# Scores for the row maximum in two 64-row halves of the array, two units at a time

## The reference

```python
q_lat = einsum('bqhd,hdl->bhql', q, k_eff)            # 16 heads of 8, latent 64
attn  = softmax(causal(q_lat @ c_kv.T / sqrt(8)))
y     = einsum('bhql,hld->bqhd', attn @ c_kv, v_eff)
g     = silu(sum over the 2 best of 8 experts: gate * (gelu(xn w1 + b1) w2 + b2))
x     = x + y * g
```

## Time and profile before

| | us |
|---|---|
| median of 3 runs | 772.93 (767.08 to 774.23) |
| the profiled execution | 773.25 |
| its span, first to last instruction | 771.5 |
| iteration 1 (maximum only) | 41.2 to 95.4 |
| iteration 2 | 95.4 to 160.4 |
| iterations 4 to 7, each | about 82 |
| the exponentials without maxima begin | 648 |

### The profile page before, as it was taken

How to read it: one execution, slowest core, us unless ns; L and a number is a source line. 1 busy time by engine, 2 the same in 40 slices (tenths; PEclk the granted TensorE clock), 3 DMA queues, 4 the chain that set the end, 5 groups by cost and what they waited for, 6 DMA issues and landing times.

```text
span 771.5 us, 14463 instructions
## 1 busy us (share of the span) xinstructions
PE 663.5 (86%) x5682; PEld 458.5 (59%) x5734; DVE 448.1 (58%) x1044; ACT 369.3 (48%) x688; POOL 234.9 (30%) x356
## 2 busy tenths in 40 slices
PE   4177698979999899989998999899998998896875
PEld 2034365537666676657665876576666775555663
DVE  5466357555857576576758575758575654425331
ACT  3502346744556455644556455645564556571210
POOL 5703001222333153124404331423331502224431
PEclk9999889979999999999999999999999999999995
DMA  2732730450035102530044004400341000000000
GB/s 71 135 62 53 120 58 8 98 95 7 8 82 97 36 1 66 88 68 1 28 100 85 8 7 103 105 7 7 87 87 27 2 7 15 21 2 0 1 14 14
DMA packets 31283, 36.31 MB, mean 47 GB/s; under 512 B 4385, under 2 KB 26512, under 8 KB 31216
## 3 DMA queue, kind: packets, MB, share of 16 engines
q1 hardware_dynamic: 31216, 35.39, 22.1%
HBM read 24.44 MB, written 9.96 MB: 45 GB/s over the span
## 4 chain that ended last, share of the span: by engine, by line
PE 64%; DVE 17%; DMA 6%; issue 4%; ACT 4%; POOL 3%; SPq 2%; another core or an unknown queue 0%; POOLq 0%; DVEq 0%; ACTq 0%
PE ps_s L804 8%; PE ps_v L824 8%; PE ps_e L789 5%; DVE cand L1264 5%; DMA kst<-split_scratch 4%; PE ps_a L749 4%; PE ps_e L786 4%; PE ps_c L890 3%; PE ps_c L903 3%; PE ps_a L738 3%; PE ps_a L713 3%; PE ps_s L808 2%; DVE stats L1195 2%; PE ps_c L907 2%; DVE second L1209 2%
## 5 line engine op out<-in xcount | busy, mean ns | idle before, releaser
L1264 DVE TENSOR_REDUCE cand<-ps_s 128x4 f32<-128x512 f32 (+1 forms) x320 | 212.9, 683 | 94.0 <-PE ps_s L808 73.8
L1069 ACT ACTIVATE prob<-ps_e 128x512 f32<-128x512 f32 x320 | 188.2, 597 | 136.8 <-PE ps_e L789 97.2
L804 PE MATMUL ps_s<-kst,qst 96*128 96x128 bf16 (+1 forms) x1024 | 134.2, 249 | 41.8 <-DMA kst<-split_scratch 23.6
L804 PEld LDWEIGHTS ps_s<-kst,qst 96*128 96x128 bf16 x1024 | 81.0, 105 | 100.7 <-issue 52.4
L789 PE MATMUL ps_e<-qst,kst 128*128 128x128 bf16 (+3 forms) x460 | 104.5, 296 | 0.0
L824 PE MATMUL ps_v<-prob,vaug 128*32 128x512 f32 (+3 forms) x1024 | 89.0, 443 | 0.3
L786 PE MATMUL ps_e<-identb,negmask 128*128 128x256 bf16 (+1 forms) x320 | 83.3, 260 | 6.0 <-ACT prob L1069 5.8
L624 POOL TENSOR_TENSOR second<-second,upmask 128x512 f32<-128x512 f32 x42 | 53.1, 1274 | 34.6 <-PE ps_c L890 34.6
L789 PEld LDWEIGHTS ps_e<-qst,kst 128*128 128x128 bf16 x512 | 50.6, 99 | 5.6 <-issue 0.3
L587 POOL CAST mparts<-nm 128x32 bf16<-128x32 f32 x16 | 3.4, 212 | 157.9 <-DVE nm L1271 157.9
L890 PE MATMUL ps_c<-second 128*128 128x128 f32 x336 | 46.0, 280 | 1.0 <-DVE second L1319 1.0
(11 more groups left out here) (301 smaller groups left out, 1076.6 us busy)
## 6 DMA issues: line engine op xcount, KB each, us to landing
qst<-split_scratch SPq DMA_DIRECT2D x48, 192.0 KB
kst<-split_scratch SPq DMA_DIRECT2D x144, 64.0 KB
split_scratch<-qparts SPq DMA_DIRECT2D x8, 384.0 KB, 2.5
split_scratch<-kparts SPq DMA_DIRECT2D x8, 384.0 KB, 2.5
xn<-in_L_attn_x_dram SPq DMA_DIRECT2D x8, 256.0 KB, 3.1
x_res<-in_L_attn_x_dram SPq DMA_DIRECT2D x8, 256.0 KB, 6.8
out_dram<-second SPq DMA_DIRECT2D x7, 256.0 KB, 2.4
max_scratch<-mrow SPq DMA_DIRECT2D x16, 96.0 KB, 1.7
```

The source lines that it names most:

```text
L804: last = mm(ps_s[:, bank, w * n:w * (n + 1)], q[0:MAXROW, hd, tok(i)], k[0:MAXROW, hd, keys[0]:keys[1]], start=(n == 0), stop=True, skip_g ...
L1069: af(prob[:, u, :], ps_e[:, u % 2, :], ACT.Exp).then_inc(S["e_emptied"], 1)
L1264: vec.tensor_reduce(cand[:, i, h0:h0 + len(hds), S_SLOT[u]], ps_s[:, u % 2, :].rearrange("p (a c) -> p a c", a=len(hds)), AX_X, ALU.max)\
```

## The change

The 16 heads are put in two sides of 8 slots. A head of side 0 has its 72 product rows from row 0 up, a head of side 1 from row 64 up, the last 8 of them wrapped to rows 0 to 7. The row maximum is taken from 64 of the 72 rows (the product of the two lowest parts is left out there): side 0 in rows 0 to 63 of the array, side 1 in rows 64 to 127, into different banks. The coarse mask is gone; the diagonal blocks get their whole mask from four matmuls of 64 rows, over 512 and 256 columns on each side, with swapped copies of the identity and the mask. A unit becomes a pair of banks: one `tensor_reduce` or one exponential over 128x1024 for both, and both banks must be empty before PE fills the next pair. Pairs for the maximum stand at even places of the plan, pairs for the exponential at odd ones. `pv` and `yt` run twice for a sequence instead of four times, each for 8 heads, two of which share 32 columns. `prob` is a ring of 6 pairs. `load_stacks` issues 25 transfers for 8 heads, of rows half as long.

```diff
 PLAN = {
-    (0, 6): ["pv0", "c_xn2t", "ln3_stats", "c_out", "gb2"], (0, 7): ["ln3_norm"], (0, 8): ["gb3"], (0, 9): ["pv1", "c_ht"],
+    (0, 6): ["c_xn2t", "ln3_stats", "c_out", "gb2"], (0, 7): ["ln3_norm"], (0, 8): ["gb3"], (0, 9): ["pv0", "c_ht"],
...
-    (3, 9): ["pv1", "c_u2"], (4, 0): ["m_parts1", "gelu", "stacks1"], (4, 1): ["pv2"], (4, 2): ["v"], (4, 3): ["yt", "x1"],
+    (3, 9): ["c_u2"], (4, 0): ["pv2", "m_parts1", "gelu", "stacks1"], (4, 2): ["v"], (4, 3): ["yt", "x1"],
...
-                        if step < GROUPS:
-                            unit(cur, nxt, step, u)
+                        if step < STEPS:
+                            pair = UNITS // 2 * (step % 2) + u // 2
+                            unit(cur if u % 2 else None, nxt if u % 2 == 0 else None, step // 2, pair)
...
-                for s in range(PARTS):
-                    sp.dma_start(qst[b.parity][n3 * s:n3 * s + n3, heads, :].rearrange("p h q -> p (h q)"), q_rows,
-                                 max_dma_last_dim=4096).then_inc(loaded, 16)
-                    for r in range(PARTS):
-                        lo = n3 * s + HD * r
-                        sp.dma_start(kst[b.parity][lo:lo + HD, heads, :].rearrange("p h q -> p (h q)"), k_rows[HD * s:HD * s + HD, :],
+                for side in range(SIDES):
+                    s0 = slot_of(half, side, 0)
+                    heads, span = slice(s0, s0 + GH), slice(TOK * s0, TOK * (s0 + GH))
+                    for lo, n, first in STACK_ROWS[side]:
+                        sp.dma_start(qst[b.parity][lo:lo + n, heads, :].rearrange("p h q -> p (h q)"), q_rows[first:first + n, span],
                                      max_dma_last_dim=4096).then_inc(loaded, 16)
+                    for pair in range(PARTS * PARTS):
+                        lo, s = (HALF * side + HD * pair) % P, pair // PARTS
+                        sp.dma_start(kst[b.parity][lo:lo + HD, heads, :].rearrange("p h q -> p (h q)"), k_rows[HD * s:HD * s + HD, span],
+                                     max_dma_last_dim=4096).then_inc(loaded, 16)
...
-            def s_unit(b, grp, u):
+            def s_pair(b, fill, u):
...
-                after(pe, S["s_emptied"], b.count(GROUPS * UNITS, UNITS * grp + u - 1))
+                after(pe, S["s_emptied"], b.count(UNIT_PAIRS, UNITS * fill + u))
...
+                    for side in range(SIDES):
+                        rows, slot = low_rows(side), slot_of(fill, side, hh)
+                        last = mm(ps_s[:, side, w * n:w * (n + 1)], q[rows, slot, tok(i)], k[rows, slot, keys[0]:keys[1]],
+                                  start=(n == 0), stop=True, skip_group_check=True)
                 if u < NT:
-                    for lo in range(0, P, FINE):
-                        last = mm(ps_s[lo:lo + FINE, bank, :].rearrange("p (a c) -> p a c", a=GH)[:, :, lo:lo + FINE],
-                                  identb[0:FINE, 0:FINE], bcast(negmask[0:FINE, 0:FINE], 1, GH), start=False, stop=True,
-                                  skip_group_check=True)
+                    for a in range(2):
+                        for side in range(SIDES):
+                            last = mm(ps_s[:, side, :].rearrange("p (n c) -> p n c", n=GH)[:, :, HALF * a:P],
+                                      half_of(identb, ident_swap, a, side),
+                                      bcast(half_of(negmask, neg_swap, a, side)[:, HALF * a:P], 1, GH), start=False, stop=True,
+                                      skip_group_check=True)
...
-                act.wait_ge(S["e_filled"], cur.count(GROUPS * UNITS, UNITS * grp + u + 1))
...
-                af(prob[:, u, :], ps_e[:, u % 2, :], ACT.Exp).then_inc(S["e_emptied"], 1)
...
+                af(prob[:, u % PROB_RING, :, :], ps_e[:, :, :], ACT.Exp).then_inc(S["e_emptied"], 1)
```

More of the change, by code:

```diff
@@ L146, in count, with head_of, slot_of, low_rows @@
         return self.c * per + k
+def head_of(fill, side, hh):
+    return FH * fill + SIDES * hh + side
+def slot_of(fill, side, hh):
+    return HALF_HEADS * side + GH * fill + hh
+def low_rows(side):
+    return slice(HALF * side, HALF * side + HALF)
 def a_number(b, n):
@@ L522, in masks @@
                 chain(g.memset(vaug[:, :, :, :], 0.0))
-                chain(g.memset(vaug[:, :, :, HD:HD + 1], 1.0))
+                for odd in range(FILLS):
+                    chain(g.memset(vaug[:, :, odd:HEADS:FILLS, FW * odd + HD:FW * odd + HD + 1], 1.0))
                 chain(g.memset(pick[:, :, :], 0.0))
@@ L686, in settle @@
                 pe.wait_ge(S["masks_ready"], 1)
-                pe.wait_ge(S["coarse_loaded"], 64)
             def a_fill(b, n):
@@ L773, in e_unit, with e_pair @@
+            def e_pair(b, fill, u):
                 q, k = qst[b.parity], kst[b.parity]
-                bank = u % 2
-                after(pe, S["e_emptied"], b.count(GROUPS * UNITS, UNITS * grp + u - 1))
-                if grp % 2 == 0 and u == 0:
-                    pe.wait_ge(S["mrow_loaded"], b.count(32, 8 * grp + 16))
+                after(pe, S["e_emptied"], b.count(UNIT_PAIRS, UNITS * fill + u))
+                if u == 0:
+                    pe.wait_ge(S["mrow_loaded"], b.count(64, 32 * fill + 32))
@@ L787, in e_unit @@
-                for hh, j, at in todo:
-                    hd = GH * grp + hh
-                    last = mm(ps_e[:, bank, at:at + TOK - P * j], k[:, hd, tok(j)], q[:, hd, P * j:TOK],
-                              start=False, stop=True, skip_group_check=True)
+                apart = 3 if u < 8 else 2
+                for side in range(SIDES):
+                    diag = ps_e[:, side, :].rearrange("p (n c) -> p n c", c=P)[:, 0:apart * (len(todo) - 1) + 1:apart, :]
+                    mm(diag, negmask[:, :], bcast(identb[:, :], 1, len(todo)), start=True, stop=False, skip_group_check=True)
+                    for hh, j, at in todo:
+                        slot = slot_of(fill, side, hh)
+                        last = mm(ps_e[:, side, at:at + TOK - P * j], k[:, slot, tok(j)], q[:, slot, P * j:TOK],
+                                  start=False, stop=True, skip_group_check=True)
@@ L821, in pv @@
                 for j, u0, at in (((0, 0, 0),), ((1, 4, 0), (3, 4, 384)), ((2, 8, 0),))[piece]:
-                    for hh in range(GH):
-                        u, o = (u0 + hh, at) if j != 2 else (u0 + hh // 2, 256 * (hh % 2))
-                        last = mm(ps_v[32 * hh:32 * hh + 32, P * j:TOK], vaug[:, j, GH * grp + hh, :],
-                                  prob[:, u, o:o + TOK - P * j], start=(j == 0), stop=(j == 2), skip_group_check=True)
+                    for side in range(SIDES):
+                        for hh in range(GH):
+                            u, o = (u0 + hh, at) if j != 2 else (u0 + hh // 2, 256 * (hh % 2))
+                            last = mm(ps_v[32 * hh:32 * hh + 32, P * j:TOK], vaug[:, j, head_of(fill, side, hh), :],
+                                      prob[:, u % PROB_RING, side, o:o + TOK - P * j], start=(j == 0 and side == 0),
+                                      stop=(j == 2 and side == SIDES - 1), skip_group_check=True)
@@ L986, in prepare @@
                 for stack in (qst, kst):
-                    af(stack[1][64:P, :, :].bitcast(F32), ident[64:P, 0:1].unsqueeze(2).to_broadcast([64, HEADS, TOK // 2]),
-                       ACT.Copy, scale=0.0).then_inc(S["stack_zeroed1"], 1)
+                    for side in range(SIDES):
+                        rows = low_rows(1 - side)
+                        af(stack[1][rows, HALF_HEADS * side:HALF_HEADS * (side + 1), :].bitcast(F32),
+                           ident[rows, 0:1].unsqueeze(2).to_broadcast([HALF, HALF_HEADS, TOK // 2]), ACT.Copy, scale=0.0)\
+                            .then_inc(S["stack_zeroed1"], 1)
                 act.wait_ge(S["loaded"], LOADED)
```

194 lines of the change are left out of this document (95 added, 99 removed), and 19 rows, old and new, of tables (LAST_PLAN, PLAN).

## The result

The changed kernel takes 792.87 us (median of 4 runs, 792.65 to 793.55), the kernel before 770.22 beside it: a ratio of 1.029 (1.025 to 1.032), slower by 2.9%. I had forecast 763.5, and 744 to 789 for 8 in 10. The profiled execution has a span of 791.1 us against 771.5, 19.6 more.

What follows compares the result with a forecast made beforehand. PE was taken to bound steady iterations, other things the ends. From 773.25 us: 7.7 off for steady iterations, 7.5 loads, 1.0 first kparts, 2 clock; 4.5 added for iteration 1, 4 for the last: 763.5, range 744 to 789.

Steps and rivals of the forecast that it cites:

- One bank pair for each kind: PE refills a pair only once all was read: 0.2 us a steady iteration, 0.8 for each pair without cover.
- rival A: Score matmuls on PE: the two 64-row halves run one after the other, giving 791.5 us; chance 0.18.
- Streaming: Maximum's scores and masks on PE: halves run together, saving 0.3 us off the diagonal and 2.0 on it an iteration.
- `pv` and `yt`: Fewer visits on PE in a steady iteration: 1.2 us saved for the first, 0.9 for the second.
- (a): Step 0: the doubled pv0, moved to (0, 9), no longer hides behind DVE's long norm; 1.0 us lost an iteration.
- (d): At (2, 0): the first reduction is twice as long and begins later, lengthening PE's wait; 0.65 us lost an iteration.
- (b): Step 0: three pairs of reductions precede the norm instead of five units, the first filled later; 0.5 us lost an iteration.
- (c): At (4, 0): pv2 waits for the exponential of the pair at (3, 9); 0.9 us of waiting an iteration.
- The loads: First half of the stacks arrives in 12.6 us instead of 15.1 in iterations 0 to 2: 7.5 us saved.
- The clock: PE's gap before iteration 3 shrinks, so the clock may stay up: 2 us saved.
- Iteration 1: Only maxima run there; fill, reduction and signals in series take 2.5 us a pair in step 0: 4.5 us lost.
- the waits take the gain: Rival: halves stream together, but loads land no sooner and the single bank pair costs more; 773 us, chance 0.21.

Runs made afterwards that it cites:

- experiment 1: The changed kernel, with pairs of exponentials in the last iteration going by turns into two bank pairs: 781.72 us, ratio 1.013.
- experiment 10: The changed kernel with the gates alone moved one place later, from (1, 4) to (1, 5): 782.37 us, ratio 1.014.
- experiment 3: The changed kernel plus eight matmuls that only fill PE's wait for the second norm in step 0: 790.72 us, ratio 1.025.
- experiment 5: The kernel before, with each transfer of a half of the stacks cut in two by heads: 769.51 us, ratio 0.997.
- experiment 2: The changed kernel, with pairs for the maximum in iteration 1 going by turns into two bank pairs: 782.75 us, ratio 1.015.
- experiment 9: The changed kernel with gates later, POOL's power for the first norm earlier and lev_d3 ahead of yt: 774.57 us, ratio 1.004.

## Why the prediction was wrong

The step that failed is "One bank pair for each kind", costed at 0.2 an iteration and 0.8 for each bare pair, with its consequence in the last iteration, "for some 6 of 20 pairs without pieces between them: 4 lost". Measured: 14.3 lost in the last iteration; a second bank pair alone shortens the stretch from its first exponential to its last from 55.5 to 45.6 us (experiment 1). Of the 14.3 the exponentials' stretch made 10.7 and the rest behind it 3.6. The mechanism was named, and its price for one pair right (1.95 forecast, 1.94 measured); the count was wrong. In place of 6 bare pairs, 11 fills waited (9.7 us) and all 6 pieces of `pv` (6.9 us): a piece of 1 us between two pairs covers only a part of 1.3 us, and `pv` now also stood right behind the pair that it reads. In the steady iterations I looked for cover on PE only (0.7 us or more between two pairs) and not at what stands ahead of the pair in the queue of the engine that empties it: the gates' exponential on ACT. Moving that one piece gave 10.5 us back, some 9 of them in the iterations where it stands (experiment 10), where the forecast had 0.2 in each of seven.

The measured time is close to rival A's 791.5. That is chance: A's mechanism isn't what happened, as the first point below shows.

The rest, by the prediction's parts. For the work of PE I take, in the timelines at full clock, the time from the start of each block to the next, without the waits, over a steady iteration of the kernel before and one of experiment 3 (its filler left out):

- Streaming: rival A is refuted. Off the diagonal a pair of 64-row matmuls takes 0.32 us (rows below) where two units took 0.44; on it 0.65 against 0.98. The 0.33 between the two is for the masks, 768 columns on each side: side by side they would take 0.33 at the pace of 512 columns in 0.22, one after the other 0.66. The halves run together. In all 13.2 us became 9.7: 3.5 saved, with 2.3 forecast.

```profile
155.23 0.40 PE L813 MATMUL ps_s<-kst,qst 64*128 64x128 bf16 x8
...
155.88 0.50 PE L795 MATMUL ps_e<-identb,negmask 128*128 128x128 bf16 x2
...
386.51 1.11 PE L904 MATMUL ps_c<-second 128*128 128x128 f32 x8
387.56 0.39 PE L813 MATMUL ps_s<-kst,qst 64*128 64x256 bf16 x4
387.88 1.13 PE L747 MATMUL ps_a<-xnT,w1s 128*128 128x512 f32 x2
388.84 1.05 PE L921 MATMUL ps_c<-second 128*128 128x128 f32 x8
389.73 0.27 PE L795 MATMUL ps_e<-identb,negmask 128*128 128x256 bf16 x1
```

- `pv` and `yt`: 1.0 and 1.0 saved, with 1.2 and 0.9 forecast. But the other blocks of PE together took 3.0 longer (the levels' products 0.85, `c_u` 0.47), so of 4.4 only 2.5 came. Most of the 3.0 is the change of tile shape, which shows up in the neighbours. In the rows above eight products of 128x128 between blocks of full shape take 0.89 (388.84 to 389.73), and eight with a 64-row block behind them 1.05 (386.51 to 387.56); over the iterations it is 0.99 to 1.13. The block behind a 64-row block is longer too: 0.96 for L747 (387.88 to 388.84), where the same product took 0.86 before (386.08 to 386.94). Nearly all blocks that grew stand next to a 64-row block. So the streaming term was mis-sized as well: 3.5 less 3.0 is 0.5 saved in an iteration and not 2.3, because a visit to the 64-row shape costs more than the 0.20 that I had added for it.
- Waits (a) to (d) and the bank pair: 3.3 forecast. PE's waits were 4.8 in the steady iteration before and 7.1, with 1.7 of filler in one of them, in that of experiment 3: 4.0 more. The sum is near, the places are not: in step 0, (a) and (b), the waits and the filler were 1.9 more, with 1.5 forecast; (c), 0.9 forecast, was 0.2; (d), 0.65 forecast, was 0.7, but as 1.56 at `lev_a4` and 0.26 on the reduction, where 1.11 had been; the bank pair, 0.2 forecast, came as 0.95 at the gates, where PE had waited 0.30 near by; and 0.6 more came at places that I hadn't named. So -2.5 + 4.0 = 1.5 in place of -1.1 (the iterations differ by 1.35), and on top of it the clock, 0.7 to 1.8 in each iteration from the fourth on, which I had named as a thing that would make the forecast wrong and not priced. Over iterations 4 to 8 this made 11 us more (-5.7 to +5.3 against the kernel before) where 5.5 less was forecast.
- The loads: -7.5 forecast. Iteration 1 began 10.8 us after the first issue and iteration 2 12.0 (12.6 forecast), where the kernel before shows 14.6 and 15.1; iteration 3 began after 12.3 without a wait, where it had been 16.2 with 5.3 of waiting. That is 3.7, 3.1 and 3.9 sooner: right in direction, and 3 us more than forecast in all. The reason given (issues that spread over 8.5 us) holds for a part (experiment 5). The landing of `kparts` in 2.53 us was right.
- The clock was at 1.00 in iteration 3 (0.94 before), as forecast, but the 2 us taken for it and the 1.1 of the iteration itself didn't come: it took 80.6 us instead of 81.1.
- Iteration 1: 4.5 lost forecast; 5.5 measured ahead of the first stack load of iteration 2. Right, and yet the wrong question: with the banks used by turns the stage gains (experiment 2).

My chances gave "the waits take the gain" 0.21 and priced it at 773, since it took 0.3 an iteration for the bank pair. The price was at fault more than the chance.

## What to carry to other kernels

Merging two small hand-overs between engines into one large one removes the overlap inside the pair: before it, ask for each pair what the consumer does between "full" and "empty", in the consumer's own queue, small instructions that wait for a third engine included. Count the bare places from the written order one by one, at both ends of the kernel first, where the other kind of work is missing and its buffers lie free; there they can be lent. A block of another tile shape is paid for in its neighbours' time too, so count it from the block before to the block behind. And a change that looks slower may still be worth having once its consequences are dealt with: here it was 2.9% slower as it came, and 3.4% faster once the order was redone and the banks lent at both ends. Compare such a kernel with the one before after the same care: against the kernel before in a new order the gain is 2.1%, and the one run with a new order but no lent banks (experiment 9) shows none.

## What the runs showed of the hardware

- Two tiles of 64 rows, each writing to banks of its own, stream side by side: 768 columns on each side add 0.33 us to a block, the time of 768 columns at the pace of 512 in 0.22. The visit to the 64-row shape costs some 0.10 in the block itself, 0.10 in the block behind it and 0.10 to 0.24 in the block ahead of it (0.99 to 1.13 for eight products that take 0.89 otherwise). The Trainium skill, TensorEngine Tiling (Array Packing), Gotcha 1, says that row tiles must write to different banks, so they need more PSUM; here each side has its own bank of the pair, and the second bank is the one that the turn had used.
- The same DMA rate (130 and 132 GB/s) kept the engines busy for 0.86 and for 0.43 of the time in the two kernels. That this is by where in the tile it landed isn't shown.
- The four parts of a norm on DVE (128x128 each) take 1.11 us with no POOL product over 128x512 beside them, 1.29 with one for the first 0.44 us (experiment 9), 2.06 with 1.20 us of one and 2.39 with 1.72. The last is the norm that PE waits 2.27 us for in step 0; the rows below, both of the changed kernel, are that norm and the same one in iteration 3, without a product. The Trainium skill, SBUF — State Buffer, in its section on the bandwidth-pool intuition, says that GpSimd and a VectorE operation on two ports can't run at once. The lengths fit in the main (0.95 longer for 1.20 of overlap, 1.28 for 1.72), whether this norm is such an operation isn't shown, and no run moved a product by itself.

```profile
162.15 1.11 DVE L1231 TENSOR_SCALAR second<-x,mv,rstd 128x128 f32<-128x128 f32 x4
...
413.00 2.39 DVE L1231 TENSOR_SCALAR second<-x,mv,rstd 128x128 f32<-128x128 f32 x4
```

- Eight matmuls that compute nothing, put in a wait of 2.27 us, kept the granted clock at 1.00 in each steady iteration and gave back 0.7 to 1.8 us; in iteration 2, where there was no such wait, the clock fell from 0.94 to 0.89 with them and 4 us were lost.
